# Graph kernel: edge attributes as two float32r halves, squares kept in PSUM, smaller DMA scratch, three engines reordered

## What is computed

```
h  = relu(layernorm(x))
m  = [h[dst], h[src]] @ W_pre.T + b_pre            # one message per edge
mx, mn, s1, s2 = max, min, sum of m, sum of m*m over the edges of each receiver
mean = s1 / deg;  std = sqrt(relu(s2/deg - mean*mean) + 1e-5)
agg  = [mx, mn, mean, std]
x1 = x + ([h, agg, agg*log(deg+1), agg/log(deg+1)] @ W_post.T + b_post) @ W_lin.T + b_lin
h2 = relu(layernorm(x1))
y  = x1 + relu([h2, mean of edge_attr over the edges of each receiver] @ W1 + b1) @ W2 + b2
```

## Time and profile before

| | before |
|---|---|
| median of 3 runs (lowest, highest) | 1425.65 us (1424.48, 1427.43) |
| the profiled execution | 1425.24 us |
| its span, first to last instruction | 1423.4 us |
| mean granted TensorE clock | 0.979 |
| edge pass, from about | 547 us |
| busy: TensorE, VectorE, ScalarE, GpSimd | 96%, 91%, 82%, 72% |

### The profile page before, as it was taken

The page is one execution under the profiler, slowest core; times in us unless marked ns, Lnnn a source line. Parts: engine busy times, 40 slices in busy tenths (PEclk is TensorE's granted clock), DMA queues, the critical chain, the costliest instruction groups (busy, mean ns, idle before and its releaser), DMA issues.

```text
span 1423.4 us, 34524 instructions
## 1 busy us (share of the span) xinstructions
PE 1360.6 (96%) x8403; PEld 1186.2 (83%) x8403; DVE 1294.2 (91%) x4180; ACT 1165.3 (82%) x2813; POOL 1029.6 (72%) x1281
## 2 busy tenths in 40 slices
PE   4899999999999997899999999999999999999994
PEld 3799999999999985788888888888888888888883
DVE  6999999999999994899999999999999999999981
ACT  2799999999999984688888888888888888888872
POOL 1777777777777776577787777777777777777722
PEclk8799999999999998999999999999999999999997
DMA  3455555555555584434444434444544444444300
GB/s 102 164 200 206 206 201 204 206 206 203 201 203 197 207 280 134 107 114 120 131 135 127 123 122 126 123 126 129 146 131 127 128 127 126 126 127 135 119 17 12
DMA packets 128443, 210.96 MB, mean 148 GB/s; under 512 B 19711, under 2 KB 66042, under 8 KB 128395
## 3 DMA queue, kind: packets, MB, share of 16 engines
q1 hardware_dynamic: 105450, 161.83, 35.7%
q0 software_dynamic: 21952, 47.55, 10.8%
q10 hardware_dynamic: 992, 1.05, 0.3%
HBM read 123.96 MB, written 90.27 MB: 150 GB/s over the span
## 4 chain that ended last, share of the span: by engine, by line
PE 88%; issue 5%; DVE 3%; POOL 2%; DMA 1%; ACT 1%; SPq 0%; POOLq 0%; DVEq 0%; ACTq 0%
PE bank L547 13%; PE bank L587 9%; PE bank L588 9%; PE bank L591 9%; PE bank L556 6%; PE bank L686 5%; PE bank L674 5%; PE bank L572 3%; PE bank L573 3%; PE bank L574 3%; PE bank L530 3%; PE bank L538 3%; PE bank L647 3%; PE bank L649 3%; PE bank L612 1%
## 5 line engine op out<-in xcount | busy, mean ns | idle before, releaser
L587 PE MATMUL bank<-comb_lo,agg_hi 128*128 128x384 f32 x784 | 276.8, 353 | 0.8 <-ACT bank L878 0.8
L588 PE MATMUL bank<-comb_hi,agg_hi 128*128 128x384 f32 x784 | 264.0, 337 | 0.0
L591 PE MATMUL bank<-comb_hi,agg_lo 128*128 128x384 f32 x784 | 263.9, 337 | 0.0
L417 POOL DMA_INDIRECT rows<-table,index x196 | 205.7, 1050 | 60.8 <-issue 60.8
L455 POOL DMA_INDIRECT y<-nout,index x196 | 200.8, 1024 | 50.8 <-issue 50.0
L417 POOL DMA_INDIRECT hs<-table,index x196 | 190.8, 973 | 56.5 <-issue 56.5
L384 POOL TENSOR_TENSOR runs<-rows,b_all 128x512 f32<-128x512 f32 x98 | 125.8, 1283 | 112.3 <-DVE rows L1058 112.3
L547 PE MATMUL bank<-w_sb,nut 128*128 128x128 f32 x1568 | 200.8, 281 | 0.8 <-ACT nut L795 0.7
L547 PEld LDWEIGHTS bank<-w_sb,nut 128*128 128x128 f32 x1568 | 182.8, 192 | 19.5 <-issue 10.6
L777 ACT ACTIVATE nh<-rows,nms,nrs 128x128 f32<-128x128 f32 x392 | 161.7, 483 | 1.3 <-DVE nms L1031 0.7
L400 POOL TENSOR_SCALAR rows<-nx,nmv,nrs 128x128 f32<-128x128 f32 x196 | 153.9, 794 | 0.0
(11 more groups left out here) (177 smaller groups left out, 3611.8 us busy)
## 6 DMA issues: line engine op xcount, KB each, us to landing
table<-rows SPq DMA_DIRECT2D x98, 512.0 KB, 3.4
nx<-in_x SPq DMA_DIRECT2D x98, 256.0 KB, 2.8
y<-nout SPq DMA_DIRECT2D x98, 256.0 KB, 2.0
inv<-inv_row SPq DMA_DIRECT2D x49, 256.0 KB, 4.7
keepm<-keepm_row SPq DMA_DIRECT2D x49, 256.0 KB, 5.4
attr<-in_edge_attr SPq DMA_DIRECT2D x48, 256.0 KB
keep<-keep_row SPq DMA_DIRECT2D x49, 128.0 KB, 3.6
reset<-reset_row SPq DMA_DIRECT2D x49, 128.0 KB, 4.4
```

The costliest lines, as they stand in the source:

```text
L417: pool.indirect_dma_start(out=to[:, s, j, :], out_offset=None, in_=of, in_offset=bass.IndirectOffsetOnAxis(ap=column(which, c, j), axis=0) ...
L587: pe.matmul(acc[:, 0:SCALERS * P], hi, w_lo, start=False, stop=False, skip_group_check=True)
L588: pe.matmul(acc[:, 0:SCALERS * P], hi, w_hi, start=False, stop=False, skip_group_check=True)
L591: mm = pe.matmul(acc[:, 0:SCALERS * P], lo, w_hi, start=False, stop=(a == SD), skip_group_check=True)
```

## The change

- The attributes' fp32 product in `hidden` becomes three float32r products, of the weights' high and low part and of the aggregated attributes' high and low part (low x low is left out, as with h2). ScalarE makes the high part (`attr_high`), VectorE the low part (`attr_low`), once a chunk; setup makes the weights' parts by a cast and a subtraction in place of a copy.
- The squares of the messages overwrite the messages in their bank, once the scans of sum, maximum and minimum are done; the squared mean then overwrites the squares there, once `scan_squares` is done. `bsq` and `mean_b2` are gone. The scans of the messages wait for the messages themselves; `messages` waits for the variance of two chunks before.
- The scratch for the descriptors of GpSimd's DMAs is given as 8192 bytes; the default is 16384.
- The lists of TensorE, ScalarE and VectorE for an edge step are in another order. SyncE's and GpSimd's are as before.

```
@@ -640,10 +641,7 @@
-    pe.wait_ge(sem("e_max"), c - 1 + EU * i)
-    pe.wait_ge(sem("e_min"), c - 1 + EU * i)
-    pe.wait_ge(sem("e_sum"), c - 1 + EU * i)
-    pe.wait_ge(sem("e_bsq"), c - 1 + EU * i)
+    pe.wait_ge(sem("e_var"), c - 1 + EU * i)
 pe.matmul(bank[3 + c % 2][:], ws_t[:], hst[:, c % 2, :], start=True, stop=False)
@@ -671,7 +670,9 @@
 cols = slice(m * P, (m + 1) * P)
-pe.matmul(bank[b][:], w1_attr[:, cols], run_attr[:, c % 2, :], start=True, stop=False)
+pe.matmul(bank[b][:], w1a_lo[:, cols], attr_hi[:, c % 2, :], start=True, stop=False)
+pe.matmul(bank[b][:], w1a_hi[:, cols], attr_hi[:, c % 2, :], start=False, stop=False)
+pe.matmul(bank[b][:], w1a_hi[:, cols], attr_lo[:, c % 2, :], start=False, stop=False)
 pe.matmul(bank[b][:], w1_lo[:, cols], h2t[:, c % 2, :], start=False, stop=False)
@@ -691,27 +692,23 @@
 have, ahead, behind = edge(k), edge(k + 1), edge(k - 1)
 if k == 0:
     open_sums()
-if have:
-    turn_attr(k, i)
 if edge(k + 2):
     turn_sender(k + 2, i)
+    turn_receiver(k + 2, i)
 if have:
     layer0(k, 0, i)
-if edge(k + 2):
-    turn_receiver(k + 2, i)
-if have:
     layer0(k, 1, i)
-if edge(k + 2):
-    messages(k + 2, i)
+    turn_attr(k, i)
 if behind:
     turn_normed(k - 1, i, not edge(k + 2))
 if have:
     layer0(k, 2, i)
+    layer0(k, 3, i)
 if behind:
     hidden(0, 7, k - 1, i)
     hidden(1, 1, k - 1, i)
-if have:
-    layer0(k, 3, i)
+if edge(k + 2):
+    messages(k + 2, i)
 if behind:
     outputs(k - 1, i)
@@ -839,10 +836,10 @@
 def message_squared(c, i):
-    act.wait_ge(sem("e_b_psum"), c + 1 + EU * i)
-    if c >= 2:
-        act.wait_ge(sem("e_sqsum"), c - 1 + EU * i)
-    act.activation(bsq[:, c % 2, :], bank[3 + c % 2][:], ACT.Square).then_inc(sem("e_bsq"), 1)
+    act.wait_ge(sem("e_max"), c + 1 + EU * i)
+    act.wait_ge(sem("e_min"), c + 1 + EU * i)
+    act.wait_ge(sem("e_sum"), c + 1 + EU * i)
+    act.activation(bank[3 + c % 2][:], bank[3 + c % 2][:], ACT.Square).then_inc(sem("e_bsq"), 1)
@@ -858,9 +855,8 @@
 act.wait_ge(sem("e_mean_b"), c + 1 + EU * i)
-if c >= 1:
-    act.wait_ge(sem("e_var"), c + EU * i)
-act.activation(mean_b2[:], mean_b[:], ACT.Square).then_inc(sem("e_mean_b2"), 1)
+act.wait_ge(sem("e_sqsum"), c + 1 + EU * i)
+act.activation(bank[3 + c % 2][:], mean_b[:], ACT.Square).then_inc(sem("e_mean_b2"), 1)
@@ -890,6 +886,12 @@
+            def attr_high(c, i):
+                act.wait_ge(sem("e_attr_run"), c + 1 + EU * i)
+                if c >= 2:
+                    act.wait_ge(sem("e_u_psum"), 2 * (c - 1) + 2 * EU * i)
+                act.activation(attr_hi[:, c % 2, :], run_attr[:, c % 2, :], ACT.Copy).then_inc(sem("e_attr_hi"), 1)
+
             def variance_pos(c, i):
@@ -902,42 +904,44 @@
 have, ahead, behind = edge(k), edge(k + 1), edge(k - 1)
 if k == 0:
     seed(0, 0, i)
+if behind:
+    squares(k - 1, i)
 if have:
     seed(k, 1, i)
-if behind:
-    squares(k - 1, i)
 if edge(k + 2):
     sender_turned(k + 2, i)
     receiver_turned(k + 2, i)
 if behind:
     spread(k - 1, i)
 if ahead:
-    high_part(MX, "e_max", run_max[:, (k + 1) % 2, :], k + 1, i)
+    message_squared(k + 1, i)
+    high_part(MN, "e_min", run_min[:, (k + 1) % 2, :], k + 1, i)
 if behind:
     normalise(k - 1, i)
 if have:
     seed(k, 2, i)
+if ahead:
+    high_part(ME, "e_mean_b", mean_b[:], k + 1, i)
 if behind:
     normed_turned(k - 1, i)
-if ahead:
-    scale_attr(k + 1, i)
-    high_part(ME, "e_mean_b", mean_b[:], k + 1, i)
-    mean_squared(k + 1, i)
-    high_part(MN, "e_min", run_min[:, (k + 1) % 2, :], k + 1, i)
 if have:
     seed(k, 3, i)
+if ahead:
+    mean_squared(k + 1, i)
+    scale_attr(k + 1, i)
+if have:
+    attr_high(k, i)
+if ahead:
+    high_part(MX, "e_max", run_max[:, (k + 1) % 2, :], k + 1, i)
+    variance_pos(k + 1, i)
+    deviation(k + 1, i)
 if behind:
     hidden(0, 7, k - 1, i)
-    hidden(1, 1, k - 1, i)
 if ahead:
-    variance_pos(k + 1, i)
+    high_part(SD, "e_std", var[:], k + 1, i)
 if behind:
     out_bias(k - 1, i)
-if ahead:
-    deviation(k + 1, i)
-    high_part(SD, "e_std", var[:], k + 1, i)
-if edge(k + 2):
-    message_squared(k + 2, i)
+    hidden(1, 1, k - 1, i)
 if ahead:
     if k >= 0:
         seed(k + 1, 0, i)
@@ -1115,7 +1119,8 @@
 last.then_inc(sem("comb_lo_out"), 1)
-dve.tensor_copy(w1_attr[:], w1_sb[:, 1, :])
+after(dve.tensor_copy(w1a_hi[:], w1_sb[:, 1, :]))
+dve.tensor_tensor(w1a_lo[:], w1_sb[:, 1, :], w1a_hi[:], ALU.subtract)
 after(dve.tensor_copy(w1_hi[:], w1_sb[:, 0, :]))
@@ -1213,13 +1218,14 @@
 if c >= 2:
-    dve.wait_ge(sem("e_u_psum"), 2 * (c - 1) + 2 * EU * i)
+    dve.wait_ge(sem("e_attr_hi"), c - 1 + EU * i)
+    dve.wait_ge(sem("e_attr_lo"), c - 1 + EU * i)
 dve.tensor_tensor_scan(run_attr[:, b, :], keepm[:, s, :], bank[2][:], run_attr[:, 1 - b, end] if c else 0.0,
...
 b, s = c % 2, c % 4
-dve.wait_ge(sem("e_bsq"), c + 1 + EU * i)
+dve.wait_ge(sem("e_b_psum"), c + 1 + EU * i)
 dve.wait_ge(sem(f"e_masks_in{s}"), 80 * (c // 4 + 1) + 80 * i)
@@ -1262,8 +1268,15 @@
                     dve.wait_ge(sem("e_sq_mean"), c + EU * i)
-                dve.tensor_tensor_scan(run_sq[:, b, :], keep[:, s, :], bsq[:, b, :],
+                dve.tensor_tensor_scan(run_sq[:, b, :], keep[:, s, :], bank[3 + c % 2][:],
                                        run_sq[:, 1 - b, end] if c else 0.0, ALU.mult, ALU.add).then_inc(sem("e_sqsum"), 1)
+
+            def attr_low(c, i):
+                dve.wait_ge(sem("e_attr_hi"), c + 1 + EU * i)
+                if c >= 2:
+                    dve.wait_ge(sem("e_u_psum"), 2 * (c - 1) + 2 * EU * i)
+                dve.tensor_tensor(attr_lo[:, c % 2, :], run_attr[:, c % 2, :], attr_hi[:, c % 2, :],
+                                  ALU.subtract).then_inc(sem("e_attr_lo"), 1)
@@ -1284,7 +1297,7 @@
 dve.wait_ge(sem("e_sq_mean"), c + 1 + EU * i)
-dve.tensor_tensor(var[:], var[:], mean_b2[:], ALU.subtract).then_inc(sem("e_var"), 1)
+dve.tensor_tensor(var[:], var[:], bank[3 + c % 2][:], ALU.subtract).then_inc(sem("e_var"), 1)
@@ -1298,42 +1311,45 @@
 def edge_step(k, i):
     have, ahead, behind = edge(k), edge(k + 1), edge(k - 1)
+    if ahead:
+        scan_sum(k + 1, i)
+        scan_max(k + 1, i)
+        scan_min(k + 1, i)
     if edge(k - 2):
         outputs(k - 2, i)
     if ahead:
-        scan_sum(k + 1, i)
-        scan_max(k + 1, i)
+        message_mean(k + 1, i)
+    if behind:
+        factors(k - 1, i)
     if have:
         mix(k, 0, i)
-    if behind:
-        factors(k - 1, i)
     if ahead:
-        scan_min(k + 1, i)
         scan_squares(k + 1, i)
     if have:
         mix(k, 1, i)
+    if ahead:
+        square_mean(k + 1, i)
     if behind:
         normed_low(k - 1, i)
+    if have:
+        scan_attr(k, i)
     if ahead:
-        message_mean(k + 1, i)
-        square_mean(k + 1, i)
+        low_part(ME, mean_b[:], k + 1, i)
+        variance(k + 1, i)
+    if have:
+        attr_low(k, i)
+    if ahead:
+        low_part(MN, run_min[:, (k + 1) % 2, :], k + 1, i)
+    if have:
+        mix(k, 2, i)
+        mix(k, 3, i)
+        negative_mean(k, i)
+    if ahead:
         low_part(MX, run_max[:, (k + 1) % 2, :], k + 1, i)
-        low_part(ME, mean_b[:], k + 1, i)
     if edge(k + 2):
         copy_factors(k + 2, i)
     if ahead:
-        variance(k + 1, i)
-    if have:
-        mix(k, 2, i)
-        scan_attr(k, i)
-    if ahead:
-        low_part(MN, run_min[:, (k + 1) % 2, :], k + 1, i)
-    if have:
-        mix(k, 3, i)
-    if ahead:
         low_part(SD, var[:], k + 1, i)
-    if have:
-        negative_mean(k, i)
 run_passes(dve, node_step, edge_step, first_step=-1)
@@ -1347,7 +1363,7 @@
-nc = bacc.Bacc("TRN2", target_bir_lowering=False, num_devices=1)
+nc = bacc.Bacc("TRN2", target_bir_lowering=False, num_devices=1, dynamic_dma_scratch_size=8192)
 arrays, args = {}, []
```

More of the change, by code:

```diff
@@ L100, in build @@
     w2_sb = sb("w2_sb", [P, 2, P])
-    w1_attr = sb("w1_attr", [P, HID])
+    w1a_hi = sb("w1a_hi", [P, HID], F32R)
+    w1a_lo = sb("w1a_lo", [P, HID], F32R)
+    attr_hi = sb("attr_hi", [P, 2, CHUNK], F32R)
+    attr_lo = sb("attr_lo", [P, 2, CHUNK], F32R)
     b1_col = sb("b1_col", [P, 2])
@@ L183, in build @@
     hdt = sb("hdt", [P, 2, CHUNK])
-    bsq = sb("bsq", [P, 2, CHUNK])
     run_max, run_min, run_sum, run_sq, run_attr = (runs[:, q] for q in range(5))
@@ L187, in build @@
     mean_b = sb("mean_b", [P, CHUNK])
-    mean_b2 = sb("mean_b2", [P, CHUNK])
     var = sb("var", [P, CHUNK])
@@ L662, in hidden @@
             def hidden(m, b, c, i):
-                pe.wait_ge(sem("e_attr_run"), c + 1 + EU * i)
+                pe.wait_ge(sem("e_attr_hi"), c + 1 + EU * i)
+                pe.wait_ge(sem("e_attr_lo"), c + 1 + EU * i)
                 pe.wait_ge(sem("e_h2t"), c + 1 + EU * i)
```

## The result

The changed kernel takes **1413.24 us** (median of 4 runs, 1412.15 to 1414.52) against 1426.21 us before in the same session (4 runs, 1424.48 to 1427.43): ratio 0.991, 95% interval 0.9895 to 0.9925. The prediction was 1415.0. The profiled execution took 1414.52 us with a span of 1412.7 us, so this span is 10.7 us shorter, the very size that was predicted; by the medians the gain is 13.0 us. The experiments show that either is made of other terms than the prediction's sum had.

The account below looks back on a forecast made before the run. TensorE bounds the kernel at 16.81 us a step; VectorE was to become the pace at 16.6. 46 x (16.6 - 16.81) = -9.7, +0.5, 0, -1.5 make -10.7 us: about 1415 us, range 1409 to 1430.

Parts of the forecast that it names:

- Part 1: TensorE, two `hidden` blocks: fp32 pairs removed (-1.72 us), six float32r products added (+1.39): -0.33 us a step, to 16.48.
- Part 2: VectorE: own length 15.85 us, plus 0.61 for `attr_low` and 0.12 before `negative_mean`, taken as 16.6 us a step.
- Rival 1: TensorE stays the pace, VectorE's own length falling below 16.48 us: 16 us less, 1409.5 us; chance 0.12.
- The PSUM sources: Two VectorE inputs move from SBUF to PSUM: 13 ns each, +0.03 us a step; by the skill, about 1421 us.
- Part 3 and 4: ScalarE needs 14.6 us a step; the loop from scans through `normalise` to messages takes 16.26 us, so doesn't bind.
- Rival 2: The loop through `normalise` and the turn of h2 becomes the pace: step 17.0 us, about 1433 us; chance 0.20.
- Rival 3: VectorE's length is right, but small waits of 0.1 to 0.2 us remain each step: 16.75 us, 1422; chance 0.17.
- Part 5, GpSimd: GpSimd's order is unchanged; its 16.33 us a step stay under 16.6, still waiting 0.3 us for the mixed rows.
- Part 5, the scratch: Halved scratch for GpSimd's gathers: cost taken as 0, with two or three transfers under way; at most 16 us a step.
- Part 6: Setup, first edge steps and last steps: +0.5, 0 and -1.5 us.
- First edge steps: `message_squared(0)` behind chunk 1's senders, about +0.6 us; first `scan_min` earlier, about -0.6: 0, between -1 and +1.
- Last steps: Step 47 +0.7 us; step 48's reordered blocks take 3.1 us off before the last turn of h2: together -1.5.

Follow-up runs that it names:

- the halves alone: Kernel before, its engine order and SBUF squares kept, with attributes as two float32r halves and the 8192-byte scratch: 1410.13 us, again 1410.05 us.
- VectorE lighter: Changed kernel with `attr_low` made only for the first two chunks, 0.60 us less VectorE work a step: 1409.97 us, step 16.48 us.
- squares in SBUF: Changed kernel with the squares of the messages and the squared mean in SBUF tiles again, one buffer each: 1410.80 us, step 16.55 us.
- the second profile: Another profile of the unmodified changed kernel, run again as reference: span 1410.9 us, median 1412.13 us.
- the first profile: Original profile of the changed kernel, against the kernel before: span 1412.7 us, profiled execution 1414.52 us.

## Why the prediction was right, and where it was not

- **Part 1, TensorE, right.** -0.33 us a step was predicted; the step with the halves alone is 16.46 to 16.48 us, and TensorE's own length in the changed kernel is 16.48 (VectorE lighter). "The moved blocks cost the same wherever they stand" is off by 0.05 us a step with the fp32 product, by nothing that can be told with the halves.
- **Part 2, VectorE as the pace, right in kind.** 16.6 was predicted; its own length is 16.51, and the step 16.55. The friction at the turn of h2 was foreseen at some 0.1 us and is there in part of the steps. With the gain of the same counting, 16.799 - 16.554 = 0.245 us where 0.21 was predicted, 46 steps would give 11.3 us instead of 9.7. Rival 1 (TensorE stays the pace) was closer than its 0.12 says: 0.03 us part the two engines. What the prediction doesn't weigh is that its own new order brings the 0.12 us that make VectorE the pace: in the old order both engines fit into 16.46 us.
- **The PSUM sources, right in the total, wrong in the reading of the earlier trace rows.** The 13 ns there aren't the source. In the changed kernel the scan of the squares takes 1275 ns from the bank. From SBUF it takes 1280 in the same order (squares in SBUF) and 1260 in the order of before, where it stands right behind another scan (the halves alone):

```profile
L1277 DVE TENSOR_TENSOR_SCAN runs<-keep,runs,bsq 128x512 f32<-128x512 bf16 x36 | 46.1, 1280 | 0.0
...
L1281 DVE TENSOR_TENSOR_SCAN runs<-keep,runs,bsq 128x512 f32<-128x512 bf16 x36 | 45.3, 1260 | 0.0
```

  Two other scans of the changed kernel that stand behind a scan take 1254 ns, from the bank. The subtraction of the squared mean takes 680 ns from the bank, 687 from SBUF in the same order. So the price of the PSUM source is nothing that can be seen, and squares in SBUF left the step at 16.55. The Trainium skill (VectorE: DVE Perf Modes, the TRN2 errata) has 62 cycles more of fixed cost with a PSUM source, by my estimate from that page's clock 65 ns for each instruction. The measurement decides, and the 1421 us of that rule didn't come.
- **Part 3 and 4, ScalarE and the loop, right.** `attr_low` finds its high half made and the scan of sums waits for no message; even at a step of 16.01 the loop held. Rival 2, with 0.20, needed 0.55 us more in it. Rival 3 fell too: the friction left is 0.04 us a step.
- **Part 5, GpSimd, wrong in its reading.** "GpSimd still waiting for the mixed rows, 0.3 us a step" isn't there. I had taken the step less its wait, 16.81 - 0.48 = 16.33, as its length. It ran a step of 16.01 us, so 16.33 was no length that it needs; why its issues take 956 to 1131 ns in one kernel and another isn't settled.
- **Part 5, the scratch, mis-sized.** Cost 0 in the steady steps was right, at half and at a quarter. The term that was missing is at the end of the program: -2.6 us by the span, 3 us by the time.
- **Part 6, the ends, wrong, and this hid the scratch.** Setup: +0.5 predicted; the cast of the index starts 0.91 us later, but the subtractions ahead of the changed lines were already 0.54 us late in that execution, so the edit's share is 0.37. First edge steps: 0, between -1 and +1, was predicted. Up to the first full step that is right: with the setup it begins 0.13 us later in the profile without a late gather. The first full step itself takes 1.5 us more than before instead of 0.25 less. The prediction had costed `message_squared(0)` and neither TensorE's wait of 2.4 us at the first turn of h2 nor the low clock behind it; with the clock up it took 15.80 to 15.82 us at the same wait, so the clock is the 1.5 us. Last steps: -1.5 was predicted, 0 was measured. The last turn of h2 comes 35.14 us behind the scan of sums of step 47 where it came after 34.26, so it wasn't brought forward; what it lost was won behind it.

So the sum was right by errors that cancel, which is luck. Against the terms of the sum, the steady steps gave 1.6 us more and the end of the program 2.6 us more; the 46 steps as a whole gave 1.3 us less than the steady ones promise, which is the first full step, and the last steps 1.5 us less; the start was 0.4 us better. That makes 12.5 us, as in the second profile. In the first profile a late gather took 1.8 us of it again and made the 10.7 us that had been predicted.

## What to carry to other kernels

When two engines are within a few hundredths of each other, lighten each alone and then both: alone, each edit was worth about 3 us here, together 25, and only the pair showed how much lies behind them. An engine's step less its wait need not be what it needs: by that count GpSimd needed 16.33 us, and it ran 16.01. Before writing out a new order to be rid of the second engine's waits, try the change of work alone in the old one: here that was 2 to 3 us faster than the whole. Read the clock in the first steps, where a wait can cost more than its own length. And cost the end of the program too, where a reserved size that is never filled can still be paid for.

## What the runs showed of the hardware that I had not expected

- The scratch of the dynamic DMAs has a price at the end of the program: 9.15, 6.57 and 4.60 us from the last issue to the end of the span with 16384, 8192 and 4096 bytes, and 1426, 1423 and 1421 us of time. What is done there, the profile doesn't show.
- The same gathers of one chunk at the start of the edge pass kept TensorE waiting between 0.97 and 3.60 us at one place, from profile to profile. Behind the waits of 3.12 to 3.60 us the four turns took 1.11 or 1.12 us, behind those of 0.97 to 2.28 us 0.66. This moves the first output block by about 2 us and is as large as what the smaller edits were meant to win.
- A wait of 2.4 us of TensorE was followed by some 3 us at a clock of 0.50 in five profiles and by none in four, at the same place of the same order. Some 20 us earlier TensorE had waited 2.74 to 4.23 us in the five and 1.08 to 2.42 in the four. The fall cost 1.5 us in the changed kernel.
- A 128x512 scan takes 1254 to 1260 ns right behind another scan and 1270 to 1280 elsewhere; whether the source lies in PSUM or SBUF made 5 ns at the same place.
